# Edge bounds first, identity products before the tables, and three weight splits on GpSimd in a one-core graph, attention and expert layer

## The reference, cut to what matters

```python
xn  = layernorm(x)
src = concat(edge_src, loops); dst = concat(edge_dst, loops)   # sorted by dst
e = leaky_relu(s_src[src] + s_dst[dst]);  ee = exp(e - emax[dst])
alpha = ee / segment_sum(ee, dst);  out = segment_sum(alpha * h[src], dst)
y = concat(x_, out2) @ Wu + bu
```

## Time and profile before

| | |
|---|---|
| median of 3 runs | 1904.53 us (1902.96 to 1904.88) |
| the profiled execution | 1903.6 us, span 1901.9 us |
| TensorE busy | 1851.5 us, 97% of the span |
| VectorE busy | 1296.5 us, 68% |
| ScalarE busy | 654.5 us, 34% |
| GpSimd busy | 558.1 us, 29% |
| mean granted TensorE clock | 0.997 of full speed |

### The profile page before, as it was taken

How to read it: one execution, slowest core, us unless ns; L and a number is a source line. 1 busy time by engine, 2 the same in 40 slices (tenths; PEclk the granted TensorE clock), 3 DMA queues, 4 the chain that set the end, 5 groups by cost and what they waited for, 6 DMA issues and landing times.

```text
span 1901.9 us, 28584 instructions
## 1 busy us (share of the span) xinstructions
PE 1851.5 (97%) x10824; PEld 1758.4 (92%) x10824; DVE 1296.5 (68%) x2242; ACT 654.5 (34%) x1243; POOL 558.1 (29%) x441
## 2 busy tenths in 40 slices
PE   6999999999899999999999999999999999999998
PEld 4678999999899999989999999999999999999998
DVE  7987579998894323878796654454558966465548
ACT  6534238887884411225211111111341111211113
POOL 1000001210001132214355654444024455455420
PEclk9999999999999999999999999999999999999999
DMA  5433302122244210033311111111240111111314
GB/s 166 123 117 103 104 14 59 44 58 60 70 142 140 67 50 1 26 98 106 97 41 34 34 50 34 51 48 56 80 139 26 34 50 35 50 34 34 112 47 125
DMA packets 83133, 131.17 MB, mean 69 GB/s; under 512 B 7462, under 2 KB 53320, under 8 KB 82990
## 3 DMA queue, kind: packets, MB, share of 16 engines
q1 hardware_dynamic: 78430, 115.97, 20.8%
q10 hardware_dynamic: 4560, 13.31, 2.3%
HBM read 101.06 MB, written 28.20 MB: 68 GB/s over the span
## 4 chain that ended last, share of the span: by engine, by line
PE 86%; DVE 5%; ACT 5%; issue 3%; ACTq 0%; SPq 0%; DVEq 0%; DMA 0%
PE pb L809 20%; PE pa L809 17%; PE pb L1304 11%; PE pb L1284 9%; PE pa L870 5%; PE pb L1314 5%; PE pb L947 3%; PE pa L1029 3%; PE pb L1190 3%; PE pa L983 2%; PE pb L1029 2%; ACT sm L1787 1%; PE pb L817 1%; PE pb L1065 1%; ACT o1h L1813 1%
## 5 line engine op out<-in xcount | busy, mean ns | idle before, releaser
L809 PE MATMUL pa<-dw_hi,hh 128*125 128x384 f32 x608 | 156.8, 339 | 1.7 <-issue 1.1
L809 PE MATMUL pa<-dw_hi,hl 128*125 128x384 f32 x608 | 156.0, 338 | 0.0
L809 PE MATMUL pa<-dw_lo,hh 128*125 128x384 f32 x608 | 155.6, 337 | 0.0
L2713 DVE TENSOR_TENSOR hl<-tr,hh 128x448 fp32r<-128x448 f32 x144 | 152.1, 1056 | 5.0
L2711 DVE CAST hh<-tr 128x448 fp32r<-128x448 f32 x144 | 78.7, 546 | 88.2 <-ACT tr L2047 83.0
L2081 ACT ACTIVATE cp<-pb 128x448 f32<-128x448 f32 x32 | 17.4, 544 | 323.1 <-PE pb L1304 316.4
L2047 ACT ACTIVATE tr<-pb,V 128x448 f32<-128x448 f32 (+1 forms) x96 | 57.1, 597 | 198.7 <-PE pb L1284 142.1
L1492 POOL CAST dw_hi<-raw 128x768 fp32r<-128x768 f32 x48 | 49.2, 1025 | 230.7 <-PE pa L809 228.5
L870 PE MATMUL pa<-S1h,D1h 125*125 125x418 bf16 x510 | 103.4, 356 | 8.1 <-DVE S1h L2207 8.1
L809 PEld LDWEIGHTS pa<-dw_hi,hh 128*125 128x125 f32 x608 | 108.8, 185 | 2.2 <-issue 1.3
L809 PEld LDWEIGHTS pa<-dw_lo,hh 128*125 128x125 f32 x608 | 109.6, 185 | 0.0
(11 more groups left out here) (470 smaller groups left out, 5134.7 us busy)
## 6 DMA issues: line engine op xcount, KB each, us to landing
raw<-in_L_mix_fc_w SPq DMA_DIRECT2D x48, 384.0 KB, 3.4
raw<-in_L_ffn_w SPq DMA_DIRECT2D x47, 384.0 KB, 3.4
md<-md_d SPq DMA_DIRECT2D x11, 546.9 KB
md_d<-mds SPq DMA_DIRECT2D x10, 546.9 KB
raw<-in_L_mix_qkv_w SPq DMA_DIRECT2D x24, 192.0 KB, 4.2
md<-md_d ACTq DMA_DIRECT2D x8, 546.9 KB
TOK<-in_x SPq DMA_DIRECT2D x10, 336.0 KB
xn_d<-TOK SPq DMA_DIRECT2D x10, 336.0 KB
```

The lines of the kernel that those rows point to most:

```text
L809: last = nc.tensor.matmul(slot[:, c, :], x_[:, cols], w_[:, c * HD2:(c + 1) * HD2], start=(k == 0 and n == 0), stop=(k == len(blocks) - 1 ...
L2713: v.tensor_tensor(hb_lo[b][:, o:o + w], z, hb_hi[b][:, o:o + w].bitcast(fp32), ALU.subtract).then_inc(sem("h_lo"), 1)
```

## The change

Three edits, and the order of two semaphore parts that goes with one of them (`e_row` and `v_tr` share one semaphore that counts up).

1. TensorE: the three bounds products move ahead of the three vector transposes. Before them come four products of the identity with itself into an unused PSUM bank, and after the transposes five more.
2. The low parts of `Wu` pages 0, 1 and 2 are made by GpSimd behind its constants, no longer by VectorE. GpSimd waits for ScalarE's high part of each page.
3. VectorE makes the low parts of pages 3 to 5 where it did, with an added wait on the common count.

```diff
-        follow("pe_once", ("e_bb", 1), ("e_tr", 1), ("v_tr", 1), ("e_row", 1), ...)
+        follow("pe_once", ("e_bb", 1), ("e_tr", 1), ("e_row", 1), ("v_tr", 1), ...)
...
             last.then_inc(sem("e_tr"), 1)
+            def idle_products(n):
+                for _ in range(n):
+                    nc.tensor.matmul(pa[:, 3, 0:P], ident[:], ident[:], start=True, stop=True, skip_group_check=True)
+
+            idle_products(4)
+            pe.wait_ge(*at("e_bc", 1))
+            nc.tensor.matmul(pb[0:1, 3, 0:NT], RM["bc"][:, 0:1], ident[0:NT, 0:NT], start=True, stop=True)
+            nc.tensor.matmul(pb[0:1, 3, 16:16 + NT], RM["bc"][:, 2:3], ident[0:NT, 0:NT], start=True, stop=True)
+            nc.tensor.matmul(pb[0:1, 3, 32:32 + NT], RM["bc"][:, 2:3], tri[:], start=True, stop=True).then_inc(sem("e_row"), 1)
             pe.wait_ge(*at("v_in", 16 * (len(VROWS) + len(VROWS2) + 1)))
             (the three vector transposes, then_inc v_tr)
-            pe.wait_ge(*at("e_bc", 1))
-            (the same three bounds products)
+            idle_products(5)
...
 GpSimd, behind the constants:
+            for k in range(3):
+                i = PG_WU + k
+                pool.wait_ge(*at("bw_hi", i + 1))
+                g_.tensor_tensor(wu[k][1][:], raw[i % NRAW][:], wu[k][0][:].bitcast(fp32), ALU.subtract).then_inc(sem("bw_split"), 1)
...
 VectorE:
-            for k in range(2):
-                page_low(PG_WU + k, wu[k])
...
-                for k in {0: (2,), 3: (3, 4, 5)}.get(t, ()):
+                for k in range(3, KT) if t == 3 else ():
+                    dve.wait_ge(*at("bw_split", PG_WU + k))
                     page_low(PG_WU + k, wu[k])
```

More of the change, by code:

```diff
@@ L243, in follow @@
                 before += n
-        follow("pe_once", ("e_bb", 1), ("e_tr", 1), ("v_tr", 1), ("e_row", 1), ("tb0", 1), ("tb1", 1), ("r_log", 1), ("r_gb", 1))
+        follow("pe_once", ("e_bb", 1), ("e_tr", 1), ("e_row", 1), ("v_tr", 1), ("tb0", 1), ("tb1", 1), ("r_log", 1), ("r_gb", 1))
         follow("pe_rows", ("wt_mm", NT), ("g_mm", 2 * NT), ("kv_mm", 2 * NT), ("qg_mm", QJOBS), ("pj_mm", NT))
@@ L839, in _ @@
             nc.tensor.transpose(pb[0:C2, 0, 2 * P:2 * P + 2], vst[0:2, 2 * P:2 * P + C2], ident[0:2, 0:2]).then_inc(sem("v_tr"), 1)
-            pe.wait_ge(*at("e_bc", 1))
-            nc.tensor.matmul(pb[0:1, 3, 0:NT], RM["bc"][:, 0:1], ident[0:NT, 0:NT], start=True, stop=True)
-            nc.tensor.matmul(pb[0:1, 3, 16:16 + NT], RM["bc"][:, 2:3], ident[0:NT, 0:NT], start=True, stop=True)
-            nc.tensor.matmul(pb[0:1, 3, 32:32 + NT], RM["bc"][:, 2:3], tri[:], start=True, stop=True).then_inc(sem("e_row"), 1)
+            idle_products(5)
             turns = {}
```

## The result

| | median | range, runs |
|---|---|---|
| before | 1904.63 us | 1902.52 to 1906.73, 20 |
| after | 1907.74 us | 1906.12 to 1909.53, 20 |

The ratio is 1.0018, with a 95% interval from 1.0011 to 1.0024: by the medians the change costs 3.1 us (2.1 to 4.6 by the interval), under 0.2%. The prediction was 1905.2 with a range up to 1907.6: it had the direction right and the size wrong, and the median lies just above the range. The profiled execution after took 1908.1 us (span 1906.4), 4.5 us over that of before.

The account below looks back on a forecast made before the run. TensorE, busy 97% of the span, was taken to bound the kernel; -0.25 (bounds), +2.7 (turns) and -1.78 (clock) gave +0.7 us at table 0's end, so 1905.2 us, range 1902.2 to 1907.6.

Parts of the forecast that it names:

- Bounds: Ahead of table 0: bounds products start at 10.78 us, 0.25 earlier, and `bnd` ends at 11.29.
- Turns: First one-hots of table 0: VectorE and GpSimd alternate by whole instructions, holding two long one-hots, +2.7 us.
- an addition: Table 0's start: if the short one-hot (D1h) takes turns as well, +0.4 us more.
- The rival without turns: Table 0: one-hots run unhindered beside GpSimd's subtractions, -1.7 to -2.0 us, 1902.6 us; chance 0.18.
- Clock ahead of table 0: Table 0's products: identity products keep TensorE busy, so its clock is up by the first product, -1.78 us.
- a rival's ground: Ahead of table 0: sparse TensorE work from 14.8 to 17.0 us may leave the clock low; that rival's chance 0.24.
- ScalarE's chain to table 2: From table 0 to table 2: ScalarE's unbroken work passes any move of table 0's end (+0.7 us) on to the end.
- the third subtraction: End of table 0's one-hots: moving its 0.9 us to GpSimd only lengthens VectorE's 0.68 us wait for the square root.
- The sum: End of table 0: -0.25 (bounds), +2.7 (turns), -1.78 (clock) make +0.7 us, carried to the kernel's end; chance 0.48.
- turns and a clock that isn't up: Table 0: one-hots are held and the 1.78 us of clock not won, +2.5 us, 1907.2 us; chance 0.24.
- Stages behind 80 us: After 80 us: lengths stay as before; a difference that isn't a plain shift would make the prediction wrong.
- SyncE's third page load: SyncE's queue: the third load comes loose at about 16.5 us instead of 26.9, with nothing won.

Follow-up runs that it names:

- e2: Kernel before with only the three weight subtractions moved to GpSimd: 1907.95 us against 1903.93, ratio 1.002.
- e7: Kernel before with only the bounds products moved first, no identity products, subtractions on VectorE: 1903.17 us against 1903.89, ratio 0.9996.
- e1: Changed kernel with the three weight subtractions back on VectorE, bounds order and identity products kept: 1904.28 us against 1903.93 before, ratio 1.0001.
- e5: Changed kernel with two subtractions on GpSimd, the third on VectorE behind table 0: 1904.85 us against 1903.89 before, ratio 1.0006.
- e6: Changed kernel with two extra GpSimd subtractions ahead of the third, five in all: 1910.96 us against 1903.89 before, ratio 1.0037.
- e3: Changed kernel with ten identity products instead of five behind the vector transposes: 1906.48 us against 1903.93 before, ratio 1.0014.
- e4: Changed kernel with fourteen identity products added ahead of table 2: 1906.19 us against 1903.93 before, ratio 1.0011.
- e9: Kernel before with only eleven identity products added ahead of table 2: 1903.81 us against 1903.73, ratio 1.0.
- e8: Changed kernel with subtractions back on VectorE and eleven identity products added ahead of table 2: 1901.41 us against 1903.89 before, ratio 0.9986.
- e11: Changed kernel, subtractions back on VectorE, eleven identity products ahead of table 2, that version's second timing: 1901.82 us against 1903.73 before, ratio 0.9988.
- e10: Changed kernel, subtractions on VectorE, eleven identity products ahead of table 2, ten instead of five behind the transposes: 1902.97 us against 1903.73 before, ratio 0.9993.

## Why the prediction was wrong, point by point

**Bounds.** Predicted 10.78 and `bnd` by 11.29; measured 10.72 and 11.24. Right. Its worth, booked at 0.25 us, was nothing beside GpSimd's subtractions (e2) and 0.3 us at table 0's end without them (e7).

**Turns.** The mechanism was right, down to each one-hot waiting for a whole subtraction, and D1h takes turns too, which the prediction had only as an addition. The second half was forecast at 17.04 us (17.4 with D1h); the second S1h ended at 16.88, since GpSimd began 0.1 earlier, its three took 5.35 us together, and the first pair, not two pairs, met them. First product +2.31, where the terms of -0.25 and +2.7 made 2.45: 0.14 too much. The rival without turns is refuted by e1, e2, e5 and e6.

**Clock ahead of table 0: the step that failed.** "I take it that the clock has risen by the first product: -1.78 us." Measured -0.83: the first seven products took 555 ns at the median, and the first fast one stands at 19.50. That is 0.95 of the miss. e3, whose 54 products are all fast, puts 0.70 of it down to the low clock; the other 0.25 is the run itself, 11.29 us at full clock behind a held first pair where the sum took 11.04. By single traces, the 0.83 that was won is the identity products' but for 0.08 (e2's table against before's). The sum booked the rise on no row: in the kernel before the first fast product comes 5.6 us into the table. Its own turns make TensorE stop for 2.25 us behind the identity products, which it saw as a rival's ground; but that this stop is the cause is not shown, since even without any stop the gain is 1.06 (e1, first eight products at 555 ns). The rival's other ground, the low level after a pause of 2.7 us, has a row against it in the same trace: table 2 of before starts after 2.71 us of stop and takes 11.27 us at a clock of 1.00.

**ScalarE's chain to table 2: the other step that failed.** It was to carry table 0's end on to table 2 by its unbroken chain. ScalarE did, to 0.01 us. But the third subtraction, costed as only lengthening VectorE's wait, left it 1.48 us long, and VectorE began 0.40 late after it: +0.37. And TensorE's stop ahead of table 2 grew from 2.71 to 3.52 us and cost +0.60 of clock (won back in e4). The prediction looked at the clock in one place only.

**The sum.** Forecast +0.7; +0.95 (table 0's run), -0.14 (turns and bounds), +0.37 and +0.60 make +2.45, as the trace has it at table 2's end. The median says +3.1 [2.1, 4.6]; what lies between is not located beyond the 0.26 us before 186 us. The wording of the rival "turns and a clock that isn't up" (+2.5) gives the trace's number, though 0.97 of it comes behind table 0.

**Left as forecast.** Stages behind 80 us kept their lengths up to 205 us, within 0.3 us. Beyond, the profiles differ by more than a shift at 548 and 1404 us, which the forecast had named as a sign of being wrong; kernels without the subtractions on GpSimd differ from before in the same two places (e9, in the first also e1, in the second also e8 and e11), so it isn't the edit's doing by these rows. SyncE's third page load came loose at 16.26 (forecast 16.5), and nobody waited for it.

**Open.** Why VectorE begins 0.40 us late after a wait of 1.48 us (after, e2, e3, e4, e6) and 0.04 after one of 0.68 to 0.69 (before, e1, e5, e7 to e11) is not known; the rows only show that the two go together. Why the clock fell in a stop of 2.7 us in e1 and e5 and not in one as long in before and e7 is open as well; one profile each can't say whether that belongs to the kernel or to the execution, and the same goes for the moment of the rise in table 0.

## What to carry to other kernels

Before handing work to an idle GpSimd, look for what VectorE does in the same microseconds: each of its 16-bit one-hots here waited out a whole GpSimd instruction, and work that had cost VectorE nothing, because it lay beside register loads, cost 2.3 us at the head of the critical chain. Unread products ahead of real ones brought TensorE's clock up earlier here, but not by the first real product (e1: 1.06 us won, not 1.78), and those that ran past the arrival of the data cost more than they gave (e10). Before a sum books a clock gain, look for a row that shows the rise after such work, and compare with a kernel whose real products start at the same time (after with e2). Follow each delay to the next stop of the same engine.

## What the runs showed of the hardware

- A 125-element one-hot of 0.26 us took 1.0 us longer beside a GpSimd subtraction (1.24 to 1.27 us in after, e3 and e5; 1.11 and 1.80 in e6): the short form waits as well as the long one.
- GpSimd's subtractions lost almost nothing in the turns: three took 5.33 to 5.35 us, two 3.57.
- The profile's granted clock reads 1.00 in the windows from 14 to 20 us while products take 555 ns; from 44 to 46 us of after it reads 0.50 where they take 555. At the start of this kernel the durations are the evidence.
- The clock's rise in an untouched stretch at 1404 us came behind 4 slow products in some profiles and behind 12 in others: 3.66 or 5.10 us for the same 13 products.
- One DMA issue on ScalarE's queue at 546 to 554 us takes 0.42 us in some kernels' profiles and 1.15 to 1.62 in others', and moves everything behind it by about 1.2 us.
